# A two-layer token mixer: low parts read from PSUM banks, another order on ScalarE and POOL, and tiles at multiples of 64 bytes

## The reference, cut to what matters

```python
xn = layernorm(x)
u  = x_ssm * silu(xn @ v1.T + b)                 # computed by earlier stages, stored turned
x  = x + (u @ w2.T + w2_b) + (q(xn) @ q(w).T + bias)   # q(): blocks of 32 rounded to an FP6 grid, times their scale
xn = layernorm(x)
k  = relu(xn @ Wk.T + bk);  v = xn @ Wv.T + bv
kv = sum over tokens of k (outer) v, per head;  k_sum = sum over tokens of k
# then, for every token: q-projection, ctx/denominator, layernorm, and a gated two-matrix FFN
```

## Time and profile before

| | before |
|---|---|
| median of 3 runs | 2332.63 us |
| time of the profiled execution | 2332.52 us |
| its span (first to last instruction) | 2330.9 us |
| TensorE matmul busy | 2148.1 us, 92% |
| VectorE busy | 1595.5 us, 68% |
| ScalarE busy | 1023.5 us, 44% |
| POOL busy | 852.4 us, 37% |
| mean granted TensorE clock | 0.978 |

### The profile page before, as it was taken

How to read it: one execution, slowest core, us unless ns; L and a number is a source line. 1 busy time by engine, 2 the same in 40 slices (tenths; PEclk the granted TensorE clock), 3 DMA queues, 4 the chain that set the end, 5 groups by cost and what they waited for, 6 DMA issues and landing times. The chain is left out here.

```text
span 2330.9 us, 27638 instructions
## 1 busy us (share of the span) xinstructions
PE 2148.1 (92%) x9466; PEld 1665.1 (71%) x9466; DVE 1595.5 (68%) x2983; ACT 1023.5 (44%) x1705; POOL 852.4 (37%) x838
## 2 busy tenths in 40 slices
PE   7999998699699999999999999599999999999997
PEld 5888887244377777777877777477777887778886
DVE  5576554778677777777677776267776777766775
ACT  3445545100145454555544544264454444555442
POOL 0030000344344444444444444024343444343443
PEclk9999999799899999999999999799999999999999
DMA  3244432789422222222232221221222112222111
GB/s 139 101 142 134 142 129 104 269 294 303 167 91 73 88 76 85 79 73 89 91 101 82 73 90 51 90 86 64 96 77 82 64 64 66 97 87 68 64 37 37
DMA packets 165462, 241.40 MB, mean 104 GB/s; under 512 B 19273, under 2 KB 93257, under 8 KB 164170
## 3 DMA queue, kind: packets, MB, share of 16 engines
q1 hardware_dynamic: 162760, 231.31, 29.7%
q10 hardware_dynamic: 2562, 8.32, 1.0%
HBM read 138.86 MB, written 100.73 MB: 103 GB/s over the span
## 5 line engine op out<-in xcount | busy, mean ns | idle before, releaser
L95 PE MATMUL bank<-e_ring,e_w_hi 128*128 128x512 f32 x512 | 207.0, 404 | 17.7 <-DVE e_ring L1425 16.7
L96 PE MATMUL bank<-e_ring,e_w_hi 128*128 128x512 f32 x512 | 205.5, 401 | 0.0
L1110 PE MATMUL bank<-d_kh,d_nat 128*128 128x512 f32 x768 | 197.4, 407 | 8.5 <-DVE d_kh L1009 7.6
L97 PE MATMUL bank<-e_ring,e_w_lo 128*128 128x512 f32 x512 | 200.5, 392 | 0.0
L1425 DVE TENSOR_TENSOR e_ring<-e_mixed,e_ring 128x512 fp32r<-128x512 f32 x128 | 95.9, 749 | 151.4 <-ACT e_ring L1323 151.4
L1306 POOL TENSOR_TENSOR e_x<-e_x,e_ff 128x512 f32<-128x512 f32 x64 | 82.5, 1289 | 238.3 <-DVE e_ff L1474 238.3
L1110 PEld LDWEIGHTS bank<-d_kh,d_nat 128*128 128x128 f32 x768 | 142.0, 192 | 38.3 <-issue 9.7
L973 DVE TENSOR_TENSOR d_qt<-bank,d_qt 128x512 fp32r<-128x512 f32 x64 | 44.3, 692 | 177.7 <-ACT d_qt L875 177.7
L1354 ACT ACTIVATE e_kr<-bank 128x512 f32<-128x512 f32 x64 | 38.0, 594 | 290.7 <-PE bank L97 235.8
L1300 POOL TENSOR_TENSOR e_x<-e_x,e_beta 128x512 f32<-128x512 f32 x64 | 83.5, 1305 | 224.1 <-ACT e_y L1345 224.1
L842 POOL TENSOR_TENSOR d_kacc<-d_kacc,d_kr 128x512 f32<-128x512 f32 x64 | 82.6, 1291 | 223.4 <-ACT d_kr L902 223.4
(11 more groups left out here) (208 smaller groups left out, 6442.5 us busy)
## 6 DMA issues: line engine op xcount, KB each, us to landing
b_xg<-in_L_attn_x SPq DMA_DIRECT2D x32, 512.0 KB, 4.8
scr_v<-b_vt SPq DMA_DIRECT2D x64, 256.0 KB, 2.7
scr_z<-b_zt SPq DMA_DIRECT2D x64, 256.0 KB, 2.1
c_z<-scr_z SPq DMA_DIRECT2D x64, 256.0 KB, 2.9
c_v<-scr_v SPq DMA_DIRECT2D x64, 256.0 KB, 3.1
scr_u<-c_v SPq DMA_DIRECT2D x64, 256.0 KB, 2.3
d_x<-in_L_attn_x SPq DMA_DIRECT2D x64, 256.0 KB, 3.0
d_ut_raw<-scr_u SPq DMA_DIRECT2D x32, 512.0 KB, 3.7
```

The costliest lines, as they stand in the source:

```text
L95: eng.matmul(out, lhs[hi], rhs[hi], start=first, stop=False, skip_group_check=onto)
L96: eng.matmul(out, lhs[hi], rhs[lo], start=False, stop=False, skip_group_check=onto)
L97: return eng.matmul(out, lhs[lo], rhs[hi], start=False, stop=last, skip_group_check=onto)
L1110: mm = pe.matmul(BG[c][:, :], s[:, i, cols], r[:, j, :], start=M % NTB == 0 and i == j, stop=M % NTB == NTB - 1 and i == 1, skip_group_che ...
```

## The change

Five edits, all but the last in the stage "mix":

1. POOL: in each step scale and shift of tile N are computed before `low_u` and before the quantising of tile N+2, no longer behind them.
2. ScalarE: `high_q(N+1)` stands before `normalise_sums(N)`.
3. `low_keys` reads the keys from bank BK (one scalar_tensor_tensor: max with 0, minus the high part) in place of `kr`; `set_keys`, which overwrites that bank, now waits for the low part (`k_lo`) instead of the high part.
4. The high and the low part of the turned tile are both taken from bank BA; the copy in `xt` is only stored. TensorE now waits for `n_lo` before it writes BA again, and two waits of ScalarE go.
5. Every tile is rounded up to 64 bytes and `SBUF_END` is 229312: by the new addresses all tiles of the program begin at a multiple of 64. Those at the lower end move up by 64 bytes or more, the weights at the upper end down by 32.

```diff
--- before.py
+++ after.py
@@ -19,7 +19,7 @@
 HEADS = 16
 DENOM_EPS = 1e-6
 
-SBUF_AT, SBUF_END = 16512, 229344
+SBUF_AT, SBUF_END = 16512, 229312
 
 CHUNK = 16
 OCTET = 8
@@ -58,7 +58,7 @@
         for n in shape[1:]:
             size *= n
         at = self.at
-        self.at += (size + 31) // 32 * 32
+        self.at += (size + 63) // 64 * 64
         assert self.at <= self.end, (name, self.at, self.end)
         return self.nc.alloc_sbuf_tensor_at(name, shape, dt, offset=at)
 
@@ -853,10 +853,6 @@
         for N in range(NT + 3):
             if N >= 3:
                 add_keys(N - 3)
-            if N % 2 and N // 2 + 1 < NT // 2:
-                low_u(N // 2 + 1)
-            if N + 2 < NT:
-                prepare_tile(N + 2)
             if N < NT:
                 pool.wait_ge(stat, 3 * N + 3)
                 nc.gpsimd.tensor_tensor(keep["rstd1"][:, N:N + 1], var_eps[:, :], keep["neg_half"][:, 0:1], ALU.pow)\
@@ -864,6 +860,10 @@
                 pool.wait_ge(rstd_done, N + 1)
                 nc.gpsimd.tensor_scalar(keep["shift1"][:, N:N + 1], keep["rstd1"][:, N:N + 1], moments[N % 2][:, 0:1],
                                         -1.0, ALU.mult, ALU.mult).then_inc(norm_done, 1)
+            if N % 2 and N // 2 + 1 < NT // 2:
+                low_u(N // 2 + 1)
+            if N + 2 < NT:
+                prepare_tile(N + 2)
 
     def scalar(act):
         def high_u(pair):
@@ -891,7 +891,7 @@
         def set_keys(M):
 
             if M:
-                act.wait_ge(k_hi, M)
+                act.wait_ge(k_lo, M)
             nc.scalar.activation(BK[:, :], bk[:, :], ACT.Copy).then_inc(k_set, 1)
 
         def keys(M):
@@ -907,13 +907,12 @@
         def take_turned(M):
             act.wait_ge(n_full, M + 1)
             if M >= 4:
-                act.wait_ge(n_lo, M - 3)
                 act.wait_ge(xt_st[M // 2 % 2], M // 4 * 16)
             nc.scalar.activation(turned(M), BA[:, :].rearrange("p (k t) -> p k t", k=KT), ACT.Copy).then_inc(n_copy, 1)
-            act.wait_ge(n_copy, M + 1)
             if M >= 2:
                 act.wait_ge(k_full, M - 1)
-            nc.scalar.activation(nt[M % 2][:, 0, :, :], turned(M), ACT.Copy).then_inc(n_hi, 1)
+            nc.scalar.activation(nt[M % 2][:, 0, :, :], BA[:, :].rearrange("p (k t) -> p k t", k=KT), ACT.Copy)\
+              .then_inc(n_hi, 1)
 
         def normalise_sums(N):
             act.wait_ge(norm_done, N + 1)
@@ -952,10 +951,10 @@
                 take_turned(N - 1)
             if N + 1 < NT:
                 set_sums(N + 1)
+            if N + 1 < NT:
+                high_q(N + 1)
             if N < NT:
                 normalise_sums(N)
-            if N + 1 < NT:
-                high_q(N + 1)
             if N + 3 < NT:
                 normalise_input(N + 3)
             b = finishing(N + 1, 0)
@@ -976,8 +975,8 @@
         def low_n(M):
             dve.wait_ge(n_hi, M + 1)
             tile = nt[M % 2]
-            nc.vector.tensor_tensor(tile[:, 1, :, :], turned(M), tile[:, 0, :, :].bitcast(F32), ALU.subtract)\
-              .then_inc(n_lo, 1)
+            nc.vector.tensor_tensor(tile[:, 1, :, :], BA[:, :].rearrange("p (k t) -> p k t", k=KT),
+                                    tile[:, 0, :, :].bitcast(F32), ALU.subtract).then_inc(n_lo, 1)
 
         def prepare_tile(N):
             tile, p = xq[N % 3], N % 2
@@ -1006,8 +1005,8 @@
 
         def low_keys(M):
             dve.wait_ge(k_hi, M + 1)
-            nc.vector.tensor_tensor(kh[M % 2][:, 1, :], kr[M % 2][:, :], kh[M % 2][:, 0, :].bitcast(F32),
-                                    ALU.subtract).then_inc(k_lo, 1)
+            nc.vector.scalar_tensor_tensor(kh[M % 2][:, 1, :], BK[:, :], 0.0, kh[M % 2][:, 0, :].bitcast(F32),
+                                           ALU.max, ALU.subtract).then_inc(k_lo, 1)
 
         def sums(N):
             p, q = N % 2, N % Q
@@ -1159,7 +1158,7 @@
                     pe.wait_ge(kv_done, HP * (2 * finishing(N, 3) + 2))
                 pe.wait_ge(xn_done, N)
                 if N >= 2:
-                    pe.wait_ge(n_copy, N - 1)
+                    pe.wait_ge(n_lo, N - 1)
                 turn_in(BA, xn[(N - 1) % 2], n_full)
             if N >= 3:
                 outer(N - 3)
@@ -1175,7 +1174,7 @@
             for step, part in ((0, sums_row), (1, values), (2, sums_column)):
                 b = finishing(N, step)
                 if b is not None and N < NT:
-                    pe.wait_ge(n_copy, N)
+                    pe.wait_ge(n_lo, N)
                     part(b)
         sums_row(B - 1)
         values(B - 1)
```

## The result

The changed kernel takes 2267.66 us (median of 4 runs, 2267.26 to 2269.19) against 2332.60 (4 runs, 2332.00 to 2332.96): ratio 0.9726, 95% interval 0.9714 to 0.9738. Its profiled execution took 2268.02 us with a span of 2266.4. Faster, as forecast (2260, range 2251 to 2280), but by 65 us, not 73.

The account below looks back on a forecast made before the run. A ring through VectorE, POOL and ScalarE, longer than TensorE's 12.05 us step, bounds "mix". Gains of 40.3, 2.5, 0.75, 27.4 and 2.1 total 73.1 us off 2332.52: 2259.4, said as 2260 us, range 2251 to 2280.

Parts of the forecast that it names:

- drain: End of the mixing pipeline: three `outer` wait for `low_keys`, each wait 0.7 us shorter, 2.1 us gained.
- second layer: `channels_out` groups save 0.5 us each, but the wait for `e_ring` grows from 1.3 to 1.8 us: gain 0.
- the addresses do nothing: Rival: the time per 12 matmuls has another cause, a mixing step needs 12.05 us, total 2270 us; chance 0.13.
- steps that keep 12.05: Sign against the forecast in "mix": steps staying at 12.05 us instead of 11.87 would show the addresses gained nothing.
- The ring through VectorE, POOL and ScalarE: In "mix", this chain of waits sets the step at about 13.1 us, above the 12.05 us TensorE needs.
- So I take the address as the cause: In "mix", multiples of 64 make TensorE's matmuls faster, 0.18 us a step, from 12.05 to 11.87 us.
- `low_u` just covered: In odd steps `low_u` behind `shift` ends 11.85 us after `w2` starts; TensorE needs it at 11.87.
- late by some tenths: Rival: `low_u` late in odd steps as POOL and VectorE block each other, 0.5 us per pair, 2275 us; chance 0.15.
- slower: Rival: `low_u` starts its own length later, even `w2` waits about 2.9 us, total 2346 us; chance 0.03.
- Even steps: `add_keys` holds L991, so `sums` comes 0.6 us late, at W+6.2 (W: start of the step's `w2`); cost 0.
- ScalarE's cover before the keys: In each mixing step ScalarE is free 0.2 us before the keys come, 11.88 against 12.07 us after `w2` starts.
- later `low_u`: 0: First mixing steps: `high_q` comes earlier and the first `low_u` later, together worth 0 us.

Follow-up runs that it names:

- e8: The kernel before with only the addresses changed, streamed and stationary tiles both at 320 modulo 512: 2332.79 us, ratio 0.9997.
- e1: The changed kernel without edit 5, so with the old addresses: 2268.51 us, ratio 0.9721.
- e2: The changed kernel with `SBUF_END` 229184, streamed upper tiles 128 bytes lower, so they and the stationary tiles begin at 320 modulo 512: 2257.48 us, ratio 0.9675.
- e6: The changed kernel with `SBUF_END` 228928, streamed tiles at 64 modulo 512, 256 apart from the stationary ones: 2257.68 us.
- e7: The changed kernel with edit 5 taken back and streamed and stationary tiles both at 288 modulo 512: 2258.91 us.
- e3: The kernel before with edits 1 and 2 alone (the new order on POOL and ScalarE), old addresses: 2276.55 us, ratio 0.9756.
- e4: The kernel before with edits 3 and 4 alone (low parts read from the banks), old order and addresses: 2271.31 us, ratio 0.9732.
- e9: The kernel before with edit 1 alone (POOL's new order): 2283.05 us.
- e10: The kernel before with edit 2 alone (ScalarE's new order): 2302.47 us.

## Why the prediction was right, and where it was off

Against the profiled execution, term by term (gain in us):

| term | forecast | measured |
|---|---|---|
| steps 3 to 35 | 40.3 | 35.9 |
| steps 35 to 38 | 2.5 | 3.1 |
| steps 38 to 42 | 0.75 | 0.1 |
| steps 42 to 63 | 27.4 | 24.6 |
| drain | 2.1 | 5.0 |
| second layer | 0 | 0.7 |
| before step 3 | 0 | -4.9 |
| sum | 73.1 | 64.5 |

The result lies in the range, but 7.7 us from the forecast and 2.3 from the rival "the addresses do nothing". The forecast's own sign against itself, steps that keep 12.05, nearly came: they take 12.01. Two misses, 7.9 us of addresses and 4.9 before step 3, are in part made good by 2.9 us of the drain that no term foresaw; that is luck.

- **The bound and the stall: right.** The ring through VectorE, POOL and ScalarE set the step, and with it gone the step is what TensorE needs. The waits of the earlier trace rows went with it, and so did the alternation of 12.40 and 13.89 us. e8 is the sharpest sign: a faster TensorE gained nothing while the ring stood.
- **Edit 5, the step that failed: "So I take the address as the cause", 0.18 us a step.** It is 0.04 (e1). Over the 57 steps of three terms that is 0.14 x 57 = 8.0 us, against 7.9 missing in them. I compared two groups that differed in two things, the multiple of 64 and the operands' distance, and took the first. The rival "the addresses do nothing" named the second in brackets and priced it at 2270; the result lies 2.3 us from it, and e2, e6 and e7 show that the distance is what counts for these matmuls. It deserved more than the 0.13 that I gave it.
- **`low_u` just covered: it holds, with 1.05 us instead of 0.02.** I saw that POOL shuts VectorE out, and used POOL's durations of before as they stood. They were long because VectorE, in turn, shut POOL out. With `low_u` starting that early, the rivals "late by some tenths" and "slower" had no ground.
- **Why VectorE is shut out: half read.** The prediction says that by the Trainium skill ("SBUF — State Buffer", Who interferes with whom) a VectorE instruction with at most one SBUF input does not contend with GpSimd. There the rule holds only outside the two-port performance modes, which the prediction left out, and the rows show a case: L991 has one SBUF input and takes 1.67 us beside `low_u`. Whether it runs in such a mode no run here shows. For the reads from a bank the rule held, 0.69 us.
- **Even steps: forecast `sums` at W+6.2, held by `add_keys`.** It came at W+5.8 in both kinds of step (1252.72 in the odd one, 1264.73 in the even one whose W is 1258.95). L990 was lengthened only to 0.32 us, because `add_keys`, begun at 1260.58 and 1.29 us long, ended 0.28 us after L990's start at 1261.59.
- **ScalarE's cover before the keys: right, but thin.** They are taken at W+0.2, and half the stall did not stay; the instruction ahead (L882) ends at 1259.04, 0.11 us before the keys at 1259.15, where I had 0.2.
- **Edits 3 and 4 were priced as helpers of the order.** I gave edit 3 the value 15 us "without it". Without both, e3 has no steady stall at all; the 8 us between e3 and e1 are the drain and an early step (13.43 us from step 3 to 4). I had not asked whether the bank reads alone would do, and they nearly do (e4).
- **The drain: 0.7 us for each of three waits is right, the clock behind them was not in the sum.** The earlier trace rows give the waits alone.
- **Second layer: nothing, right, and for the reason given, at a smaller size.** Twelve matmuls of `channels_out` take 2.77 us instead of 2.80, and the wait for `e_ring` takes it up: 1.30 us in the kernel before and in e1, with the old addresses, 1.39 in the changed kernel and in e2. I had 0.5 us a group for it. From the second on, groups are 49.6 to 49.7 us apart in every kernel of this study. The 0.7 us of the table I leave open; e1, with the old addresses, gains as much there.
- **Before step 3.** 1.3 us go between the first `w2` and step 3. There TensorE waits 6.3 us for the `low_u` that now stands behind `shift`, and in the kernel before it had other waits in that place; the term "later `low_u`: 0" was too good. The other 3.6 us come ahead of the first `w2`, in code that no edit changes but for addresses. That `w2` stood between 626.4 and 630.1 us in the fourteen traces of this study, at 626.7 in e8, which has new addresses, and at 628.8 in e9 and e10, which have the old ones. So the addresses don't explain it, and I leave the cause open.

## What to carry to other kernels

Where several edits aim at one stall, price each by what is left when the others are made: here the single edits gained 50, 31, 39 and 23 us and all together 65, because TensorE's own pace caps every step. A pace that differs between two groups of matmuls should be laid against everything in which the groups differ, the operands' places to each other too, and one constant changed and run settles it; with the ring gone, that constant (e2) was worth 11 us more, and 2257.48 us is the fastest kernel here. And durations of POOL and VectorE in a row are those beside what ran then: here both got shorter when VectorE's operand left SBUF (`low_keys` and `low_u`, `low_n` and `rstd`).

## What was not expected of the hardware

- Twelve `w2` matmuls of 512 columns take 2.72 us (227 ns each) when streamed and stationary operand start at the same place modulo 256 bytes, 2.75 at 64 apart, 2.79 at 128 and 2.80 at 224. The multiple of 64 in itself gave nothing (288 modulo 512: 2.72). The other distances weren't run, and `channels_out` and `outer` don't follow this table.
- `rstd`, one element per partition, went from 997 to 549 ns when VectorE's neighbour instruction read a bank, and `low_u` from 2848 to 2393.
- A wait ahead of twelve matmuls left them at a mean granted clock of 1.00 in eight of eight cases at 1.55 us and in none of twelve at 2.67 us, where part of them ran at 1.2 GHz; between, at 1.99 and 2.24 us, it went either way, at 1.99 in one and the same kernel.
